# A decoder kernel's norms: the first norm of two feed-forward stages computed in the end of the stage ahead, and the order of some sums in the latent attention

## What is computed

```python
x = _layernorm(x + _L0_attn_ref(x, ...))              # state-space mixer
x = _layernorm(x + _L0_xattn_ref(x, ctx_2048, ...))   # grouped attention, fp8 round trips, 361 context tokens
x = _layernorm(x + _L0_ffn_ref(x, w1, b1, w2, b2))    # ternary weights, gelu, 512 -> 2048 -> 512
x = _layernorm(x + _L1_attn_ref(x, wq, wkv_a, wkv_b, wo))   # latent attention
x = _layernorm(x + _L1_xattn_ref(x, ctx_2048, ...))   # image and text attention
x = _layernorm(x + _L1_ffn_ref(x, w_gate_up, w_proj)) # gated, group-ternary weights, silu, rms norm

def _bit_quant(w):                                    # of _L0_ffn_ref
    scale = jnp.maximum(jnp.mean(jnp.abs(w)), EPS)    # over the whole matrix
    return jnp.clip(jnp.round(w / scale), -1.0, 1.0)

def ternary_quant(w, g=64):                           # of _L1_ffn_ref: a scale for each 64 weights
    w_g = w.astype(jnp.bfloat16).reshape(-1, g)
    scale = jnp.clip(jnp.mean(jnp.abs(w_g), axis=-1, keepdims=True), 1e-08, None)
    return (jnp.clip(jnp.round(w_g / scale), -1, 1) * scale).reshape(w.shape)
```

## Time and the profile before

| | us |
|---|---|
| median of 3 runs | 2283.65 (2279.96 to 2287.03) |
| profiled execution | 2284.96, its span 2283.2, granted TensorE clock 0.98 of full |
| PE busy | 2164.9 (95%), 13328 instructions |
| PE weight load busy | 1704.1 (75%) |
| DVE busy | 1479.5 (65%) |
| ACT busy | 1174.4 (51%) |
| POOL busy | 476.3 (21%) |
| DMA | 131.66 MB at a mean of 58 GB/s |

### The profile page before, as it was taken

One profiled execution on the slowest core, in us unless ns is written; L12 is line 12 of the kernel. 1 busy time (PEld: TensorE's weight loads), 2 busy tenths in 40 slices (PEclk: granted clock), 3 DMA queues, 4 the chain that ended last, 5 costly groups with the idle time before them and its releaser, 6 DMA issues. The chain is left out here.

```text
span 2283.2 us, 35524 instructions
## 1 busy us (share of the span) xinstructions
PE 2164.9 (95%) x13328; PEld 1704.1 (75%) x13328; DVE 1479.5 (65%) x4007; ACT 1174.4 (51%) x3014; POOL 476.3 (21%) x443
## 2 busy tenths in 40 slices
PE   9998999999999999999996989999898999998998
PEld 5645788888888888888875975665655785665987
DVE  2385768777777777787666746565565557884445
ACT  2153667676767676666552334443534445772222
POOL 1210222222212222221121002232242100221432
PEclk9999999999999999999998999999999999999999
DMA  6013111001111111100002203223211420004100
GB/s 247 7 65 114 36 38 33 15 35 38 38 36 38 38 38 36 38 11 26 10 4 78 111 3 139 102 79 115 88 70 45 170 91 20 2 2 169 53 1 29
DMA packets 44772, 131.66 MB, mean 58 GB/s; under 512 B 6536, under 2 KB 21672, under 8 KB 40120
## 3 DMA queue, kind: packets, MB, share of 16 engines
q1 hardware_dynamic: 32792, 108.32, 13.0%
q0 software_dynamic: 2304, 12.58, 1.4%
q10 hardware_dynamic: 9504, 8.50, 1.3%
HBM read 108.84 MB, written 20.15 MB: 56 GB/s over the span
## 5 line engine op out<-in xcount | busy, mean ns | idle before, releaser
L782 PE MATMUL psum<-qa_kv_raw,context 128*128 128x256 f32 (+1 forms) x1536 | 343.6, 380 | 0.0
L782 PEld LDWEIGHTS psum<-qa_kv_raw,context 128*128 128x128 f32 (+1 forms) x1536 | 277.2, 184 | 44.9
L768 PE MATMUL psum<-qa_w,qa_xq 128*100 128x256 bf16 (+1 forms) x3072 | 266.8, 247 | 3.1 <-PEq L60 3.1
L768 PEld LDWEIGHTS psum<-qa_w,qa_xq 128*100 128x100 bf16 x3072 | 255.8, 126 | 4.1 <-issue 4.0
L884 ACT ACTIVATE qa_prob<-psum,qa_nm 100x361 f32<-100x361 f32 x128 | 71.9, 562 | 167.9 <-DVE qa_nm L1016 167.9
L1108 POOL TENSOR_TENSOR qa_w<-qa_w_raw,qa_w 128x768 bf16<-128x768 f32 x28 | 46.0, 1644 | 370.7 <-DVE qa_w L958 370.7
L2522 ACT ACTIVATE it_prob<-psum,it_nm 100x257 f32<-100x257 f32 (+1 forms) x256 | 101.9, 412 | 40.0 <-DVE it_nm L2547 40.0
L839 PE MATMUL psum<-qa_catq,qa_o 128*128 128x400 f32 x512 | 111.9, 361 | 9.9 <-DVE X L1055 6.0
L978 DVE BATCH_NORM_STATS2 qa_st<-psum 100x6 f32<-100x128 f32 x320 | 69.6, 284 | 78.6 <-PE psum L768 78.6
L1114 POOL TENSOR_TENSOR qa_o<-qa_o_raw,qa_o 128x512 fp32r<-128x512 f32 x32 | 40.7, 1271 | 350.4 <-DVE qa_o L966 350.4
L1007 DVE TENSOR_SCALAR qa_nrm_t<-psum,qa_mv,qa_sd 100x128 f32<-100x128 f32 x320 | 107.8, 403 | 2.4
(11 more groups left out here) (354 smaller groups left out, 5059.9 us busy)
## 6 DMA issues: line engine op xcount, KB each, us to landing
qa_w_raw<-in_qa_w SPq DMA_DIRECT2D x8, 1536.0 KB, 6.8
la_gf_raw<-in_gf_w SPq DMA_DIRECT2D x16, 768.0 KB, 4.7
gf_w<-gf_ternary SPq DMA_DIRECT2D x4, 3072.0 KB, 22.2
qa_piece<-in_tf_pieces ACTq DMA_DIRECT2D x64, 128.0 KB, 2.1
qa_o_raw<-in_qa_o SPq DMA_DIRECT2D x8, 1024.0 KB, 5.2
gf_ternary<-la_gf_made POOLq DMA_DIRECT2D x8, 768.0 KB, 3.8
gf_ternary<-gf_last_made POOLq DMA_DIRECT2D x8, 768.0 KB, 3.8
context<-in_context SPq DMA_DIRECT2D x8, 722.0 KB, 12.4
```

The costliest lines, as they stand in the source:

```text
L768: mm = pe.matmul(psum[0:T, 2 + at // 512, at % 512:at % 512 + width], xq[:, kind, k, b * T:(b + 1) * T], w3[:, s, part, k, at:at + width], ...
L782: mm = pe.matmul(psum[0:rows, i // 2, (i % 2) * 256:(i % 2) * 256 + 256], ctxT[:, k, b * TC + t0:b * TC + t0 + rows], kv_raw[:, s, k, :], ...
```

## The change

It has seven parts.

1. The norm of the first half of the ternary stage, the thresholds and the load of the Gelu table move into the end of `grouped_attention`. The projections there get banks of their own (`LAST_BANKS`, and bank 2 for one of group 0's half), so that they don't wait for `add_out`.
2. A class `TernaryEarly` fetches the first 3 of 16 pieces of raw weights (512 KB each, from an array in another order) at the end of the attention; the others follow in a ring of 8 slots. `ternary` is split into `ternary_up` and `ternary_down`, `LEAD` is 2, and the norm of the second half moves into the loop of the first half (mean at the stage's start, center at j = 0 and 1, squares at 1 and 2, variance after step 3, roots at 4, inverts at 6 and 8, high parts at 10 to 13).
3. The last scaling of the ternary stage's last norm (`nrm.scale(3, i)`) moves to the latent stage's start. The down-projection there takes the first half of the tokens first. A memset of DVE's (`k_rot`) moves to POOL.
4. In the latent quads the sums stand in another order, in three banks by piece, and DVE takes two of piece 1's scales ahead of `ternary(0)`.
5. The first half's norm of the gated stage moves into the end of the image and text attention, and the second half's into the loop of the first half.
6. Between the gated halves DVE scales chunk 0 ahead of the low part of step 0 and the others behind it; the sums into X move to j = 1, and PE waits for each chunk's scaling rather than for all sums.
7. Buffers are shared so that all this fits (`core.room`, `norm_std`, aliases of the latent weights).

The core of the diff, in the order of the program:

```diff
 grouped_attention, tensor:
-            for c in (2, 3):
-                project_out(G - 1, 0, c, last + 1 - B + c)
+            project_out(G - 1, 0, 2, last - 5)
+            project_out(G - 1, 0, 3, last - 4, 2)
             turn_probs(last)
             weigh_values((B - 1) % 2, last)
+            pe.wait_ge(S_["proj_out"], last - 3)
+            nrm.mean(pe, 0)
+            pe.wait_ge(tern.totalled, 2)
+            for i in range(2):
+                mm = pe.matmul(psum[:, 4, i:i + 1], core.ones[:, :], core.total[:, i:i + 1], start=True, stop=True)
+            mm.then_inc(tern.all_sum, 1)
             for c in range(C):
-                project_out(G - 1, 1, c, last - 3 + c)
+                project_out(G - 1, 1, c, last - 3 + c, LAST_BANKS[c])
+                if c == 1:
+                    nrm.var(pe, 0)
 vector:
             quantise(G - 1, 1, B - 1, last)
-            for c in range(C):
-                add_out(1, c, last - 3 + c)
+            for i in range(2):
+                nrm.center(dve, 0, i)
+            thresholds()
+            add_out(1, 0, last - 3, LAST_BANKS[0])
+            add_out(1, 1, last - 2, LAST_BANKS[1])
+            nrm.scale(dve, 0, 0)
+            add_out(1, 2, last - 1, LAST_BANKS[2])
+            nrm.invert(dve, 0, 1)
+            add_out(1, 3, last, LAST_BANKS[3])
...
 ternary_ffn_stage, tensor:
-            nrm.mean(pe, 0)
...
             nrm.mean(pe, 1)
-            nrm.var(pe, 0)
-            nrm.var(pe, 1)
-            pe.wait_ge(S_["scale_ready"], 1)
...
+                    if not at and j == 3:
+                        nrm.var(pe, 1)
 vector:
                     if not at and j + LEAD < FC:
-                        ternary(j + LEAD)
+                        ternary_up(j + LEAD)
+                    if not at and j + 1 < FC:
+                        ternary_down(j + 1)
+                    if not at and j in (0, 1):
+                        nrm.center(dve, 1, j)
+                    if not at and j in (6, 8):
+                        nrm.invert(dve, 1, (j - 6) // 2)
...
-            for i in range(2):
-                nrm.scale(dve, 3, i)
...
 latent_attention_stage:
-    sum_after = {3: (0, 0), 4: (0, 1), 5: (0, 2), 6: (1, 0), 7: (1, 1), 8: (1, 2), 11: (2, 0)}
+    sums_after = {3: [(0, 0)], 4: [(0, 1), (1, 0)], 5: [(0, 2), (1, 1)], 6: [(1, 2)], 11: [(2, 0)]}
+    sum_bank = {0: 7, 1: 6, 2: 7, 3: 5}
...
-            for i in range(2):
-                for h in range(2):
+            for h in range(2):
+                pe.wait_ge(nrm.normed, 6 + 2 * h)
+                for i in range(2):
...
-            dve.memset(k_rot[:, :, :], 0.0).then_inc(S_["krot_ready"], 1)
+            for i in range(2):
+                nrm.scale(dve, 3, i)
...
 image_text_attention, tensor:
-            for i in range(C, 2 * C):
-                project(i)
+            project(C)
+            pe.wait_ge(S_["proj_out"], C)
+            nrm.mean(pe, 0)
+            project(C + 1)
+            nrm.var(pe, 0)
+            project(C + 2)
+            project(C + 3)
...
 gated_ffn_stage, vector:
+                    if half and j == 0:
+                        scale_by_rms((0,))
                     dve.wait_ge(S_["hi_ready"], m + 1)
                     dve.tensor_tensor(h2[:, r, 1, :], hid[:, r, :], h2[:, r, 0, :], ALU.subtract).then_inc(S_["h2_ready"], 1)
+                    if half and j == 0:
+                        scale_by_rms((1, 2, 3))
+                    if half and j == 1:
+                        add_scaled()
```

More of the change, by code:

```diff
@@ L752, in _ @@
             sp.wait_ge(S_["kv_in"], 16 * G)
+            sp.wait_ge(S_["w_lo"], (G - 1) * C)
+            for j in range(tern.LEAD):
+                tern.fetch(sp, a, j, tern.first[:, j, :])
         @block.tensor
@@ L834, in project_out @@
                     pe.wait_ge(S_["catq_ready"], u + 4)
-                if not early(u, 1):
+                if not early(u, 1) and bank == 4:
                     pe.wait_ge(S_["proj_out"], u)
@@ L947, in _ @@
             probs_out(G * B - 1)
+            for i in range(2):
+                nrm.square(act, 0, i)
+            for i in range(2):
+                nrm.root(act, 0, i)
+            act.activation(spare[:, :], core.eps[1.0], ACT.Gelu)
         @block.vector
@@ L1183, in ternary_ffn_stage, with piece @@
         spare = sb("spare", [P, 1])
-        total, scale, half = sb("total", [P, 2]), sb("scale", [P, 2]), sb("half", [P, 4])
         parts = sb("parts", [P, 2, C, N], F32R)
-        nrm = HalfNorm(nc, core, ctx, "tf_ln", X, X, 1e-5, (6, 7, 6, None), ((2, 3), (7, 7), (7, 7), (5, 6)))
-        raw_in = [core.sem(f"tf_raw_in{i}") for i in range(4)]
         S_ = {n: core.sem(f"tf_{n}") for n in (
-            "totalled", "all_sum", "scale_ready", "half_ready", "part_hi", "part_lo", "last_mean",
-            "low_ready", "w_ready", "h_mm", "hid_ready", "hi_ready", "h2_ready", "y_all", "y_out")}
+            "part_hi", "part_lo", "last_mean", "up_low", "down_low", "up_ready", "down_ready", "h_mm", "hid_ready", "hi_ready", "h2_ready", "y_all", "y_out")}
+        core.held += [*tern.sems, *tern.raw_in]
         block = ctx.enter_context(nc.Block())
+        def piece(j):
+            r = j % tern.SLOTS
+            whole = tern.first[:, r, :] if r < tern.LEAD else ring[:, r - tern.LEAD, :]
+            return whole, whole[:, 0:D].rearrange("p (c o) -> p c o", c=C), whole[:, D:2 * D]
         def half_of(h):
@@ L1206, in _ @@
         def _(sp):
-            for q in range(4):
-                if q >= 2:
-                    sp.wait_ge(S_["w_ready"], (q - 1) * FC // 4)
-                fetch_ternary_quarter(sp, q, raws, raw_in, a)
+            for j in range(tern.LEAD, FC):
+                if j >= tern.SLOTS:
+                    sp.wait_ge(S_["up_ready"], j - tern.SLOTS + 1)
+                    sp.wait_ge(S_["down_ready"], j - tern.SLOTS + 1)
+                tern.fetch(sp, a, j, piece(j)[0])
             early.fetch(sp, a)
@@ L1331, in thresholds @@
[L1331 to L1338 removed]
+                    dve.wait_ge(S_["up_ready"], j)
@@ L1356, in _ @@
                                   ALU.subtract).then_inc(S_["part_lo"], 1)
-            for j in range(1, LEAD):
-                ternary(j)
-            for i in range(2):
-                nrm.invert(dve, 1, i)
+            ternary_up(1)
+            ternary_down(0)
             for at in range(2):
@@ L2527, in _ @@
             result_out(B - 1)
+            act.activation(spare[:, :], core.eps[1.0], ACT.Sqrt)
+            for i in range(2):
+                nrm.square(act, 0, i)
+            for i in range(2):
+                nrm.root(act, 0, i)
+            act.activation(spare[:, :], core.eps[1.0], ACT.Silu)
         @block.vector
@@ L2586, in _, with add_out @@
                 roots_out(p, c, B - 1)
-            for i in range(2 * C):
+            def add_out(i):
                 c, h = i % C, i // C
@@ L2592, in _ @@
                                          ALU.add).then_inc(S_["proj_out"], 1)
+            for i in range(C + 1):
+                add_out(i)
+            for i in range(2):
+                nrm.center(dve, 0, i)
+            add_out(C + 1)
+            nrm.scale(dve, 0, 0)
+            add_out(C + 2)
+            nrm.scale(dve, 0, 1)
+            add_out(C + 3)
         @block.gpsimd
```

298 lines of the change are left out of this document (161 added, 137 removed).

## The result

The changed kernel takes 2251.99 us (median of 4 runs, 2251.19 to 2253.20) beside 2284.17 for the kernel before in the same series (2279.96 to 2287.03). The ratio is 0.9861, with a 95% interval of 0.9844 to 0.9878: 32 us less, 42.5 were forecast. The profiled spans are 2249.3 and 2283.2, so 33.9 us are there to be divided up.

The account below looks back on a forecast made before the run. PE, busy for 95% of the span, bounds the kernel, so only its waits can give time. Terms -18.0 - 6.1 - 16.3 + 4.6 - 6.7 = -42.5 us give 2242.5 profiled, median 2241.2; range 2231 to 2256.

Parts of the forecast that it names:

- the first rival: Partial gain of 30 us (25 to 36): ternary loop bound by DVE, latent quads gain only 1.4 each; chance 24%.
- The ternary norm's move: Ternary stage's norm into the attention's end and the first loop: minus 18.0 us, bounds minus 20 and minus 15.
- Steps (a) and (b): Ternary seam at 1220.0 instead of 1222.9; then first hidden chunks at about 1225 instead of 1241.2.
- Step (c): Ternary loop with the norm inside: 53.8 us from first hidden chunk to last down-projection, which starts at 1278.9, not 1296.94.
- 2.5 us for steps that DVE and POOL stretch: Part of the ternary loop's 53.8 us: four steps of 3.53 instead of 2.92 us, as before.
- My bound of -15: Ternary norm's smallest gain, if each step carrying a center or inversion is longer by it, less 0.2 slack a step.
- The transfer rule and the table rule: Skill's 1 MiB batching and 1.38 us table-load drain; as rival, two steps lost in each loop, 2253 us; chance 2%.
- The latent start: Latent stage's start: scaling behind the seam, down-projection at full clock, 10.7 instead of 13.03 us; minus 6.1 us.
- The latent quads: Waits of the sums for scales go, scores start sooner: minus 16.3 us, bounds minus 12 and minus 22.
- The gated start: Norm's move ahead of the gated seam: seam 6.2 us later, weights' landing replaces the norm; plus 4.6 us.
- Between the gated halves: Seam between gated halves: down-projection 1 starts at 2188.5 instead of 2195.20; minus 6.7 us (minus 5 to minus 7).
- The rival on the other side: TensorE stays at 1.2 GHz in a loop; all 16 slow gated steps cost 70 us, 2311; chance 2%.

Follow-up runs that it names:

- lead3: Changed kernel with the up weights three steps ahead instead of two in the first ternary loop; 2253.04 us in a single run.
- roots_no_table: Changed kernel with the two roots in the first ternary loop run as Gelu, so both table loads go; 2253.20 us in a single run.
- split_fill: Changed kernel with the first gated weight transfer split into four and filler matmuls in the latent quads; 2236.42 us, ratio 0.9793.
- the first experiment: The run latent_old_sums: changed kernel with the latent sums in their old order and one bank; 2265.17 us, ratio 0.9904.
- gated_mid_back: Changed kernel with DVE's four scalings and additions between the gated halves ahead of the second half's first step again; 2253.75 us in a single run.
- latent_old_sums: Changed kernel with the latent sums in their old order and in one bank (7) again; 2265.17 us, ratio 0.9904.
- before_gw_split: Kernel before with only the first gated weight transfer split into four; 2285.34 us beside 2285.16.
- gated_norm_back: Changed kernel with the gated stage's norm back at its start for both halves; 2247.48 us, ratio 0.9829.
- latent_fill: Changed kernel with three matmuls that nothing reads in PE's waits behind each latent quad's last two sequences' probabilities; 2243.89 us, ratio 0.9815.
- gw_split: Changed kernel with the first gated weight transfer (3 MB) split into four of 768 KB with a semaphore each; 2245.45 us, ratio 0.9819.
- best_all: Changed kernel with split gated transfer, latent fillers and the second half's norm products in the ternary loop on DVE; 2235.63 us, ratio 0.9787.

## Why the prediction was right, and where it was off

The direction was right, and each of the five terms is in the trace with its sign. The measured 2252 lies inside the range and 11 us over the value. The gain of 32 us isn't in the band that had 60% (36 to 48) but in that of the first rival (25 to 36, 24%): the range held the result because it took in that rival. By mechanism half of the rival came true, as shown below. The profiled execution (2251.2 us) lies 8.7 us over the forecast for it. Of that 5.4 are the ternary norm's, 1.8 the latent quads', 1.4 a slower start of the text attention, and the rest small.

**The ternary norm's move: -18.0 forecast, -12.6 measured.** No run puts this norm back, so the whole is read from the traces of before and after. Steps (a) and (b) were right and a little small: -3.3 and -14.7 for -2.9 and -13.3. The -3.3 holds for this trace. Of the twelve traces of the changed kernel and its variants nine have the seam at 1219.0 to 1220.5 us and three (`lead3`, `roots_no_table`, `split_fill`) at 1222.5 to 1223.1, no sooner than before; in those the granted clock is 0.51 to 0.53 from 1202 to 1209 us, where it is 1.00 in the changed kernel's, and a part of the delay stands ahead of that already. What decides it is open. Step (c), what the loop pays for the norm inside it, failed in size. It said 53.8 us from the first hidden chunk to the last down-projection; it is 61.16. The start at low clock takes 4.35 instead of 2.9 + 0.8. Against steps of 2.92 us, the variance adds 2.37 (forecast 2.7) and the roots 1.47 (forecast 1.0). The roots' 1.0 came from a misread row: ACT's slack in a steady step of before is 1.77 us and not 2.3, which would have given 1.6.

```profile
1280.48 0.60 ACT L1296 ACTIVATE tf_hid<-psum,params 128x400 f32<-128x400 f32 x1 [1.77 <-PE psum L1220]
```

The mis-sized term is the "2.5 us for steps that DVE and POOL stretch": step by step it is 1.66 for the two centers, 2.2 for the steps with an inversion, and 5.9 for the steps with POOL's products and low parts, 9.7 in all (the last step, which has no hidden chunk, takes 2.03 and gives 0.9 back). For POOL's low parts alone 2.5 was about right; centers, inversions and products had nothing. My bound of -15 was broken too, since it took DVE's additions one by one against their durations and left out POOL. The rows for this were there: steps of 3.53 with POOL's short operations beside them (three of them and one of 3.02, not four), and a DVE with 0.19 us to spare in a step. I carried them over and didn't ask what POOL's two longer products, which had stood at the loop's first step, would do inside it. The trace of before shows their price there, on the same comparison, 2.10 us long beside the second product:

```profile
1249.33 2.10 DVE L1323 TENSOR_SCALAR tf_low_up<-tf_raw,tf_half 128x512 bf16<-128x512 f32 x1
...
1247.10 4.05 POOL L204 TENSOR_TENSOR X<-tf_ln_cen,tf_ln_std 128x800 f32<-128x800 f32 x2 [36.37 <-DVE tf_ln_std L195]
```

Cutting them gives back 3.4 us. That LEAD 2 costs nothing was right, though not for the reason that I gave: in steps 0 to 12 DVE mostly needs longer than PE, not less, and a lead of 3 changes nothing either. So the half of the first rival that was about this loop came true: DVE became its bound, at 7 us more than forecast where the rival had named 3. The prediction's own sign of being wrong showed too: PE waits for low parts (`tf_h`) in 11 of the 15 steps.

**The transfer rule and the table rule.** The ring of 512 KB pieces never held PE: the lists of waits name no transfer in the ternary loop. The roots' loads and the Gelu behind them (1239.41 to 1245.88) hold no time beyond two loads, two roots and the wait for the variance; the drain of the Trainium skill ("ScalarE: Activation LUTs", section "What ACT_TABLE_LOAD costs") doesn't show here either.

**The latent start: -6.1 forecast, -5.8 measured**, two thirds of it the seam (-3.8), one third the down-projection at full clock (-2.0).

**The latent quads: -16.3 forecast, -14.5 measured.** By quad it was -2.0, -4.7, -4.7 and -3.2 for 1.4, 4.3, 5.3 and 5.3. The removed wait is settled by the first experiment. Between quads without a dip of the clock it is worth more than forecast: 4.7 us for the first (94.73 to 90.04) and 6.1 for the third (95.77 to 89.67 in `gated_mid_back`), where the forecast had 4.3 and 5.3. What the step missed is that dip, 30 us behind the first scores. Counted over the first three quads of each trace, two of nine with the old order have it (the kernel before, `latent_old_sums`, `before_gw_split`), and 16 of 24 with the new order and no fillers, at 2.6 to 4.3 us each. So a part of the gain goes to another place in the quad, and how much differs from one execution to the next. That the new order makes the dips likelier is what these counts suggest; it isn't shown, since the counts come from few executions and repeat from one to the next.

**The gated start: +4.6 forecast, +6.0 measured between these two traces**, as +7.7, -5.0 and +3.3 for +6.2, -4.6 and +3.0. The weights' landing took the norm's place as forecast (11.3 us; 11.6 before). What the norm costs ahead of the seam was right: from the second of the eight output projections to the seam it takes 26.96 us instead of 20.68, 6.3 for 6.2. The other 1.4 of the +7.7 stand ahead of that, in the attention (171.01 us for 169.58), and aren't the norm's, since `gated_norm_back` has 171.00. In the attention's first 8 us the granted clock is 0.62 in the changed kernel and in `gated_norm_back`, and 0.80 before; `latent_fill`, with 0.81, takes 169.45. Without this the term is +4.6, as forecast. `gated_norm_back` shows the whole step as a loss, `gw_split` that the loss was in the form of the transfer.

**Between the gated halves: -6.7 forecast, -6.5 measured**, and shown to be that edit's alone.

**The rival on the other side.** No loop ran at 1.2 GHz; the gated loop took 75.77 us for 16 steps and the variance. The clock did matter, but in the latent quads, where I had looked at it only behind the big wait.

## What to carry to other kernels

Work that is moved from a seam into a loop costs what its engine has to spare in a step of that loop, and what it does to the engines beside it; before moving it, add up each engine's step, and look for operations that last longer when another engine works. When a stage's opening work is moved ahead of its seam, ask what it hid: here it hid the landing of a 3 MB transfer, and four pieces with a semaphore each turned a loss of 6 us into a gain of 2 (377.1 us from the text attention to the end in `gw_split`, 379.5 in `gated_norm_back`). Filler matmuls in a thin stretch were cheap (0.5 us a quad) and made 6 us of spread between kernels with the same code go away.

## What the runs showed that I had not expected

DVE's comparison with bf16 output (0.48 us) doesn't share time with POOL's 128x800 product: both times it started 0.27 us after it and ended 0.28 us behind it (2.12 us). It isn't the comparison alone. POOL's four low parts in this loop (L1413, 1.07 to 1.32 us) each lengthen what DVE has started beside them, twice a comparison (1.27 and 1.28 us) and twice a `scalar_tensor_tensor` of the same size, which takes 0.75 us alone:

```profile
1273.77 1.42 DVE L1361 SCALAR_TENSOR_TENSOR tf_w_down<-tf_ring,tf_half,tf_low_down 128x512 fp32r<-128x512 f32 x1
...
1273.45 1.19 POOL L1413 TENSOR_TENSOR tf_parts<-X,tf_parts 128x400 fp32r<-128x400 f32 x1 [2.84 <-ACT tf_parts L1311]
```

The same latent code took 89.7 to 90.0 us a quad with the granted clock at 1.00, and 92.2 to 94.3 where it was 0.50 for 7 to 10 us. Ahead of the falls that I looked at PE had short matmuls with waits of 0.6 us between them, and with three fillers there none of 9 full quads (`latent_fill`, `split_fill`, `best_all`) fell.
